# The lead of a transformer-layer kernel: products of ones on TensorE, and the second batch's first steps moved into it

## What is computed

```python
mod = (_silu(L0_c) @ L0_wmod).reshape(L0_c.shape[0], 6, 1, -1)
sa, ca, ga, sb, cb, gb = (mod[:, 0], mod[:, 1], mod[:, 2], mod[:, 3], mod[:, 4], mod[:, 5])
...
h = _layernorm(x, axis=-1) * (1 + ca) + sa
x = x + ga * _L0_attn_ref(h, L0_attn_wq, L0_attn_wk, L0_attn_wv, L0_attn_wo)
h = _layernorm(x, axis=-1) * (1 + cb) + sb
x = x + gb * _L0_ffn_ref(h, ...)
```

## Time and profile before

| | us |
|---|---|
| median of 3 runs | 591.85 |
| lowest, highest | 589.08, 592.23 |
| the profiled execution | 589.51 |
| its span, first to last instruction | 587.7 |
| the lead, up to the first scoreT (L876) | 48.1 |

### The profile page before, as it was taken

One profiled execution on the slowest core, in us unless ns is written; L12 is line 12 of the kernel. 1 busy time (PEld: TensorE's weight loads), 2 busy tenths in 40 slices (PEclk: granted clock), 3 DMA queues, 4 the chain that ended last, 5 costly groups with the idle time before them and its releaser, 6 DMA issues.

```text
span 587.7 us, 10308 instructions
## 1 busy us (share of the span) xinstructions
PE 556.5 (95%) x3102; PEld 308.3 (52%) x3102; DVE 371.3 (63%) x862; ACT 255.0 (43%) x519; POOL 206.6 (35%) x268
## 2 busy tenths in 40 slices
PE   4889999999999999999999999999999998999985
PEld 3453223233333333333443456557798897989664
DVE  6386577778678786788866359645344443433397
ACT  3213536664766647555477431103343443434100
POOL 6200000000030660306631753741666766666400
PEclk9976999999999999999999999999999999999998
DMA  7243117100221231311200588624455655542395
...
DMA packets 44004, 67.34 MB, mean 115 GB/s; under 512 B 9371, under 2 KB 32292, under 8 KB 43564
## 3 DMA queue, kind: packets, MB, share of 16 engines
...
## 4 chain that ended last, share of the span: by engine, by line
PE 81%; DVE 9%; issue 3%; DMA 3%; ACT 1%; POOL 1%; SPq 1%; POOLq 0%; ACTq 0%; DVEq 0%
PE ps L876 23%; PE ps L889 11%; PE ps L1107 8%; PE ps L973 7%; PE ps L1128 6%; PE ps L825 5%; PE ps L967 4%; PE ps L834 3%; PE ps L847 3%; PE ps L1093 3%; PE ps L902 3%; DVE max_q L1220 2%; PE ps L811 2%; DMA results<-y_sb,dest 1%; PE ps L932 1%
## 5 line engine op out<-in xcount | busy, mean ns | idle before, releaser
L1220 DVE TENSOR_REDUCE max_q<-ps 128x1 f32<-128x512 f32 x256 | 163.7, 685 | 71.5 <-PE ps L847 69.6
L703 ACT ACTIVATE probs<-ps 128x512 f32<-128x512 f32 x256 | 138.0, 596 | 100.8 <-PE ps L876 100.5
L847 PE MATMUL ps<-k_rows,q_rows 31*128 31x512 f32 x512 | 148.8, 673 | 2.0 <-DMA k_rows<-qk_raw 2.0
L876 PE MATMUL ps<-q_rows,k_rows 32*128 32x512 f32 x512 | 145.6, 647 | 0.9 <-DVE max_q L1220 0.9
L561 POOL DMA_INDIRECT results<-y_sb,dest x96 | 94.9, 989 | 67.0 <-issue 35.1
L876 PEld LDWEIGHTS ps<-q_rows,k_rows 32*128 32x128 f32 x512 | 41.8, 186 | 70.6 <-ACT probs L703 51.1
L1107 PE MATMUL ps<-up_sb,oT 128*128 x384 | 70.8, 327 | 2.3 <-DVE oT L1582 1.4
L889 PE MATMUL ps<-probs,v_ext 128*32 128x512 f32 x512 | 68.2, 605 | 1.1 <-ACT probs L703 1.1
L1107 PEld LDWEIGHTS ps<-up_sb,oT 128*128 128x128 f32 x384 | 61.3, 190 | 3.3 <-issue 3.2
L1128 PE MATMUL ps<-down_sb,e_hidT 96*128 x192 | 49.8, 382 | 3.6 <-ACT e_hidT L760 3.6
L1582 DVE COPY oT<-ps 128x512 f32<-128x512 f32 x48 | 33.0, 690 | 30.7 <-PE ps L1093 30.1
...
## 6 DMA issues: line engine op xcount, KB each, us to landing
...
```

What stands on the lines that cost most here:

```text
L703: act.activation(probs[:, u % 8, :], ps[:, st_bank(t.b, g, u), :], ACT.Exp).then_inc(exp_done, 1)
L847: pe.matmul(ps[:, banks[u % len(banks)], :], q_rows[32 * i:32 * i + ONE, b % 2, g, qt * P:(qt + 1) * P], k_rows[32 * i:32 * i + ONE, b % 2 ...
L876: pe.matmul(ps[:, st_bank(b, g, n), :], k_rows[32 * i:32 * i + 32, b % 2, g, kt * P:(kt + 1) * P], q_rows[32 * i:32 * i + 32, b % 2, g, :] ...
L1220: dve.tensor_reduce(max_q[:, g % 2, qt, i:i + 1], ps[:, banks[(16 * g + n) % len(banks)], :], AXX, ALU.max).then_inc(max_done, 1)
```

## The change

**Start.** PE begins with 14 products of ones by ones (of_ones), which only need the ones, now POOL's first instruction; two more stand after each of the first three column pairs of the modulation, and 8 after TP1. The results go to bank O and are never read. ACT's exp(-c) waits for c alone (c_ld). DVE clears half of q_rows, does the sigmoid, then the statistics; it normalises two of the four tiles (ACT the other two) and writes the second half of hT. POOL clears half of v_ext early, and k_rows and the other half after xn.

**Lead.** QK1's rows for group 0 are issued by ACT, not by SP. V0 is projected ahead of the first scores. Between the scores of the lead stand V1, 8 products of ones, the transposes of batch 1 (TP0+, TP1+), 4 products of ones; then QK0+ and QK1+ of batch 1, 8 products of ones, and 8 more after the last score. SP sends the maxima of group 0 ahead of the rest of wmod, and then places batch 1's first rows.

**Turn 0** loses TP0, TP1, QK0 and QK1 and has its other steps moved forward; places 7, 15, 23 and 29 are now empty.

```diff
--- before.py
+++ after.py
-    LEAD = ("TP0", "TP1", "QK0", "QK1", "QK2", "QK3", "V0", "V1", "MAX3")
-
-    FIRST = {"MAX0": 0, "TP0": 1, "TP1": 3, "QK0": 5, "QK1": 7, "MAX1": 8, "MOD0": 9, "MOD1": 11, "V0": (13, 15),
-             "MAX2": 16, "MODT": 17, "QK2": (19, 21), "QK3": (23, 25), "MAX3": 26, "V1": (27, 29), "NT0": 30, "NT1": 31}
+    LEAD = ("TP0", "TP1", "QK0", "QK1", "QK2", "QK3", "V0", "V1", "TP0+", "TP1+", "MAX3", "QK0+", "QK1+")
+
+    FIRST = {"MAX0": 0, "V0": (1, 3), "MOD0": 5, "MAX1": 8, "MOD1": 9, "QK2": (11, 13), "MAX2": 16, "MODT": 17, "QK3": (19, 21),
+             "MAX3": 24, "V1": (25, 27), "NT0": 30, "NT1": 31}
...
+    def done_in(self, lead):
+
+
+        for name, use in lead.uses.items():
+            if name.endswith("+"):
+                self.uses[name[:-1]] = use
...
+        c_ld, ones_s, v_clear, k_clear = (sem(n) for n in ("c_ld", "ones_s", "v_clear", "k_clear"))
...
+        turns[0].done_in(lead)
...
-            sp.dma_start(cT[:, :].rearrange("p (k b) -> p k b", k=KD), c_in.rearrange("(k p) b -> p k b", p=P)).then_inc(mod_ld, 16)
+            sp.dma_start(cT[:, :].rearrange("p (k b) -> p k b", k=KD), c_in.rearrange("(k p) b -> p k b", p=P)).then_inc(c_ld, 16)
...
             def turn(t):
                 max_rows(t, 0)
-                if t.pre:
+                if t.pre and not t.mod:
                     place_rows(t, 0, 0)
                     place_rows(t, 0, 1)
-                if t.mod:
-                    place_rows(t, 1, 0)
-                    place_rows(t, 1, 1)
                 max_rows(t, 1)
...
-            sp.wait_ge(consts, 3)
             sp.wait_ge(q_clear, 1)
+            place_rows(lead, 0, 0)
+            sp.wait_ge(q_clear, 2)
+            sp.wait_ge(k_clear, 1)
+            sp.wait_ge(v_clear, 2)
             sp.dma_start(k_rows[ONE:P:P // G, :, :, :].rearrange("p w g n -> p (w g n)"),
                          v_ext[0:G, :, :, :, :].rearrange("p w j h d -> p (w j h d)")).then_inc(ones_ld, 16)
-            for g in range(NG):
+            for g in range(1, NG):
                 for c in range(2):
                     place_rows(lead, 2 * (g // 2) + c, g)
+            max_rows(lead, 3)
             sp.dma_start(wmod[:, :, 2 * D:6 * D], wmod_in[:, 2 * D:6 * D].rearrange("(k p) n -> p k n", p=P)).then_inc(w_ld, 16)
             for w_d, w_s in ((wo, wo_sb), (gate, gate_sb)):
                 sp.dma_start(w_s[:, :, :], w_d.rearrange("(k p) n -> p k n", p=P)).then_inc(w_ld, 16)
-            max_rows(lead, 3)
+            for c in range(2):
+                for g in range(2):
+                    place_rows(turns[0], c, g)
             for w_d, w_s in ((sgate, sgate_sb), (sup, sup_sb), (sdown, sdown_sb)):
                 sp.dma_start(w_s[:, :, :], w_d.rearrange("(k p) n -> p k n", p=P)).then_inc(sh_ld, 16)
...
+            pool.memset(ones[:, :], 1.0).then_inc(ones_s, 1)
             st.did(pool.memset(ident[:, :], 0.0))
-            st.did(pool.memset(ones[:, :], 1.0))
...
+            pool.memset(v_ext[:, 0, :, :, :], 1.0).then_inc(v_clear, 1)
...
             deviations(0, TJ, 1)
-            pool.memset(v_ext[:, :, :, :, :], 1.0).then_inc(consts, 1)
-            pool.memset(k_rows[:, :, :, :], 0.0).then_inc(consts, 1)
+            pool.wait_ge(xn_ready, TJ)
+            pool.memset(k_rows[:, :, :, :], 0.0).then_inc(k_clear, 1)
+            pool.memset(v_ext[:, 1, :, :, :], 1.0).then_inc(v_clear, 1)
             deviations(TJ, NT, 2)
...
-            act.wait_ge(mod_ld, 32)
+            act.wait_ge(c_ld, 16)
             act.activation(ctmp[:, :], cT[:, :], ACT.Exp, scale=-1.0).then_inc(c_exp, 1)
...
             act.wait_ge(nmr_s, 1)
-            normalise(lead)
+            normalise(lead, range(2))
             act.wait_ge(modT_s, 1)
-            for k in range(KD):
-                to_hT(lead, f"TP{k}", 0)
-            for c in range(4):
-                raw_qk(lead, c)
-            for m in range(2):
-                values_out(lead, m)
-            negate_max(lead, 3)
+            to_hT(lead, "TP0", 0)
+            raw_qk(lead, 0)
+            raw_qk(lead, 1)
+            written(act, lead, "QK1")
+            act.wait_ge(k_clear, 1)
+            for i in range(G):
+                act.dma_start(k_rows[32 * i:32 * i + HD, 0, 0, :], qk_raw[32 * i:32 * i + HD, 1, :]).then_inc(rows_ld[0], 16)
+            raw_qk(lead, 2)
+            raw_qk(lead, 3)
+            values_out(lead, 0)
             act.wait_ge(nmr_s, 2)
             normalise(turns[0])
+            values_out(lead, 1)
+            for k in range(KD):
+                to_hT(turns[0], f"TP{k}", 1)
+            negate_max(lead, 3)
+            for c in range(2):
+                raw_qk(turns[0], c)
             for t in turns:
...
-            pe.wait_ge(mod_ld, 32)
+            def of_ones(times):
+
+
+                for n in range(times):
+                    pe.matmul(ps[:, O, 0:P], ones[:, :], ones[:, :], start=True, stop=True)
+
+            pe.wait_ge(ones_s, 1)
+            of_ones(14)
+            pe.wait_ge(mod_ld, 16)
             pe.wait_ge(c_ready, 1)
             for c in range(2 * KD):
                 for k in range(KD):
                     mm = pe.matmul(ps[:, 0, c * B:(c + 1) * B], wmod[:, k, c * P:(c + 1) * P], cT[:, k * B:(k + 1) * B],
                                    start=(k == 0), stop=(k == KD - 1))
+                if c < 2 * KD - 1:
+                    of_ones(2)
             mm.then_inc(modT_ps, 1)
             pe.wait_ge(consts, 1)
...
                     if b == 0 and u == 2:
-                        written(pe, lead, "V1")
+                        written(pe, lead, "QK0+")
                     above(pe, exp_done, 64 * b + u - 2)
...
             for k in range(KD):
                 tokens_to_columns(lead, f"TP{k}", 0)
+            of_ones(8)
             pe.wait_ge(qkv_ld, 48)
             for c in range(4):
                 project_qk(lead, c)
+            project_v(lead, 0)
             for n in range(16):
                 score(0, 0, n, SC + ST[0:2])
-                if n in (3, 7):
-                    project_v(lead, n // 4)
+                if n == 3:
+                    project_v(lead, 1)
+                if n == 7:
+                    of_ones(8)
+                if n == 11:
+                    for k in range(KD):
+                        tokens_to_columns(turns[0], f"TP{k}", 1)
+            of_ones(4)
             turn_max(lead, 3)
             for n in range(16):
                 score(0, 1, n, SC + ST[0:2])
+                if n in (3, 7):
+                    project_qk(turns[0], n // 4)
+                if n == 11:
+                    of_ones(8)
+            of_ones(8)
             pe.wait_ge(max_done, 32)
             pe.wait_ge(ones_ld, 16)
...
-            dve.memset(q_rows[:, :, :, :], 0.0).then_inc(q_clear, 1)
-            statistics(0, TJ)
-
+            dve.memset(q_rows[:, 0, :, :], 0.0).then_inc(q_clear, 1)
             dve.wait_ge(c_exp, 1)
             st.then(dve.tensor_scalar(ctmp[:, :], ctmp[:, :], 1.0, None, ALU.add))
             st.then(dve.reciprocal(ctmp[:, :], ctmp[:, :]))
+            dve.wait_ge(c_ld, 16)
             dve.tensor_tensor(cT[:, :], cT[:, :], ctmp[:, :], ALU.mult).then_inc(c_ready, 1)
+            statistics(0, TJ)
             minus_mean_over_deviation(0, TJ, 1)
+            dve.wait_ge(nmr_s, 1)
+            for j in (2, 3):
+                dve.tensor_scalar(xn[:, j, :], x[:, j * D:(j + 1) * D], rstd[:, j:j + 1], nmr[:, j:j + 1], ALU.mult, ALU.add).then_inc(xn_ready, 1)
             dve.wait_ge(modT_ps, 1)
-            st.then(dve.tensor_copy(modT[:, 0:KD * B], ps[:, 0, 0:KD * B]))
-            dve.tensor_scalar(modT[:, KD * B:], ps[:, 0, KD * B:2 * KD * B], 1.0, None, ALU.add).then_inc(modT_s, 1)
+            st.did(dve.tensor_copy(modT[:, 0:KD * B], ps[:, 0, 0:KD * B]))
+            st.then(dve.tensor_scalar(modT[:, KD * B:], ps[:, 0, KD * B:2 * KD * B], 1.0, None, ALU.add))
+            dve.sem_inc(modT_s, 1)
+            frees(dve.tensor_scalar(hT[:, 1, :], full(dve, lead, "TP1"), modT[:, (2 + 1) * B:(2 + 1) * B + 1], modT[:, B:B + 1], ALU.mult, ALU.add),
+                  lead, "TP1")
...
+            dve.memset(q_rows[:, 1, :, :], 0.0).then_inc(q_clear, 1)
             statistics(TJ, NT)
...
+            minus_mean_over_deviation(TJ, NT, 2)
             for n in range(16):
                 score_max(0, 0, n, SC + ST[0:2])
-            minus_mean_over_deviation(TJ, NT, 2)
             for n in range(16):
                 score_max(0, 1, n, SC + ST[0:2])
```

## The result

| us | before | after |
|---|---|---|
| median (4 runs each) | 591.79 (589.08 to 592.23) | **584.94** (584.11 to 585.91) |
| ratio after to before, 95% interval | | 0.990 (0.987 to 0.993) |
| the profiled execution; its span | 589.51; 587.7 | 584.85; 582.9 |
| first projection; first scores | 13.92; 24.50 | 13.15; 24.30 |
| first scoreT | 48.13 | 49.54 |

585.4 was forecast, 584.94 came; the sum, made against a profiled execution, gave 584.4, and the one of after took 584.85. The total hides three deviations, though: by these two traces the lead did not become 1.0 us shorter but 1.4 longer, turn 0 gave 4.8 instead of 4.1, and 1.4 us of the difference of the two spans arise after the turns, where the change touches nothing.

A forecast was written before the change was run, and what follows sets the result against it. DVE's row maxima were taken to pace the lead's scores, PE turn 0. Lead 1.0, turn 0 at full clock 2.1 and its moved steps 2.0 make 5.1 us off 589.51, 584.4; plus 1.0 gives 585.4 (8 in 10: 581.5 to 591).

The forecast's parts named there:

- The start: Lead up to first scores: ones raise PE's clock before the modulation, QK0 at 13.05 against 13.92; 2.1 us gained.
- four k rows, 4 x 0.63: Lead: ACT issues group 0's four k rows at 0.63 us each, to 19.8, landed at 21.8.
- the first scores at 22.4: Lead: first scores at 22.4 against 24.50, with V0 last; 2.1 us gained (1.3 to 2.8).
- The scores: Lead's scores: group 0 gains 0.15 us, the change of groups 0.4, group 1 with its new fillers loses 1.65.
- The clock's term: Turn 0's first places, MAX0 and TP0, at full clock: 2.1 us gained.
- The fillers' term: Turn 0 without TP0, TP1, QK0, QK1: 2.0 us gained (0 to 5.0), as empty places still wait 0.91.
- The sum: Whole kernel: 1.0 + 2.1 + 2.0 = 5.1 us off the profiled execution's 589.51, giving 584.4.
- (a): Rival, lead: the clock falls in spite of the ones, 10 us more, 595.4; chance 0.12.
- (b): Rival, start: ones don't raise the clock by the modulation, QK0 at 19.4, 6.3 us later, 591.7; chance 0.08.
- (c): Rival, turn 0: removing its four steps gives the full 5.0 us, 582.4; chance 0.10.
- (d): Rival: PE, not DVE, paces all 17 us at low clock; 8.5 us come back, not 2.5; 579.4; chance 0.03.
- (e): Rival: DVE's small steps give back turn 0's 2.0 us, ACT's issues hold V0 1.5 longer; 588.9; chance 0.10.

The follow-up runs named there:

- e4: Changed kernel with the ones row of k_rows copied early, as two DMAs ahead of group 0's q rows on SP: 582.73 us, 0.987 of before.
- e10: Changed kernel without any products of ones up to the first projection, those of the scores kept: 586.23 us in one execution.
- e6: Changed kernel once more, unchanged, for a second trace: 584.8 us (9 runs), 0.991 of before.
- e5: Kernel before once more, unchanged, for a second trace: 588.9 us (1 run).
- e7: Kernel before with only products of ones added in the lead's scores, nothing moved: 587.78 us, 0.996 of before.
- e3: Changed kernel with 8 products of ones added at each of turn 0's empty places 15, 23 and 29: 588.35 us, 0.996 of before.
- e2: Changed kernel without the products of ones between and behind the lead's scores, those of the start kept: 589.42 us, 0.996 of before.
- e9: Changed kernel with MOD0, MOD1 and MODT of turn 0 done in halves on two places each: 582.54 us, 0.986 of before.

## Why the prediction was right, and where it was not

**The start came out right up to QK0, in part by luck.** Ones before the modulation, the modulation at the fast pace, 3.3 us for it (3.2 forecast), QK0 at 13.15 (13.05). Two errors cancelled: PE could begin at 1.06 rather than 1.75 and was done with the ones at 6.4, but then it waited for wmod until 7.10. A third was hidden: the sigmoid was not done near 4.5 but at 5.57, since c landed at 4.2 and DVE's first step then took 0.65 us, and xn not by 9.6 but at 10.32. Had wmod landed at 6, QK0 would have come at 12.9 all the same, as in e4. The clock's rise within the ones was right: 28 instructions at 0.221 would be 6.2 us and took 5.36, and in e10 the projections were slow without them. Where in the ones it rises differs: they take from 4.74 us (e4) to 6.24 (e6).

**The step that failed is "four k rows, 4 x 0.63", and with it "the first scores at 22.4".** The four issues took 3.89 us, not 2.5, and the copy of QK2 behind them came at 21.36. I had named what is queued behind the issues but costed an issue by a row of before, where the same 64 KB transfer had been issued 2.7 us ahead of the first row (15.38 against 18.06) and not between the rows. e4 takes that transfer away and finds 22.32. Of the 2.1 us that the start was to give, 0.2 came (24.50 to 24.30; 1.0 by e5 and e6).

**The scores cost more than said.** From first scores to first scoreT it was 23.63 before and is 25.24: +1.6, where the sum had -0.15 - 0.4 + 1.65 = +1.1. Group 0 took 0.1 more than before (ones for V is an even swap, 0.65 behind them), the change of groups gave 0.42 (1.42 from the last maximum to the next against 1.84), and group 1 lost 1.95: the three idle times are 1.66, as forecast, and four separate groups of four maxima take 4 x 2.48 = 9.92, not 9.65.

**The clock's term was right,** 2.1 forecast and 1.9 to 2.4 by e7, which changes nothing else in turn 0. (The forecast's own terms, 6.06 us for the two places before less 3.83 less 0.3, come to 1.9 and not 2.1.) **The fillers' term too:** e7 and after both run turn 0 at the full clock and are 2.4 apart (76.3 and 73.9), against 2.0; e3 puts three of them back for 2.6.

**The sum.** The lead ends 1.41 us later, turn 0 is 4.80 shorter, so turn 1 begins 3.39 earlier:

```profile
126.86 0.27 ACT L614 ACTIVATE neg_max<-ps 16x128 f32<-16x128 f32 x1 [0.45 <-PE ps L855]
```

```profile
123.47 0.27 ACT L628 ACTIVATE neg_max<-ps 16x128 f32<-16x128 f32 x1 [0.45 <-PE ps L888]
```

These are that negation in before and in after. From here to the last MAX, both take 183.36 us, so the 3.4 are kept. The other 1.4 of the 4.8 between the spans arise in the experts' stretch and around it, and e5 shows the kernel before doing that by itself. So the change is worth 3.4 us where this pair of traces can see it, against 5.1 forecast; the other pairs, with e5 at 127.50 and e6 at 124.84, give 2.0 to 4.0. The forecast of the total was helped by chance: its sum had 1.7 us too much, 1.3 us that arise after the turns and outside the span went the same way (589.51 to 584.85 is 4.7), and of the 1.0 us added for the medians only 0.1 was needed on the side of after.

**The medians** are 5.7 to 6.9 apart, more than the traces. Each execution lists its mean granted clock. Over three comparisons the kernel before has 52 executions: 26 with a clock of 0.980 or more, median 589.4 us, and 26 below, median 591.9. Both profiled executions of it, at 0.982 and 0.979, took 589.5 and 588.9. The nine of e6 lie between 0.993 and 0.999. So slower executions of the kernel before go with a lower mean clock, and its traces, both among the fast ones, show no such execution. Whether it has further low spells, and where, stays open; a mean can't say it, since e5's lies under before's only by the tail beyond 550 us. e7 points the same way, though its interval is too wide to show it: 2.75 us by the medians (0.6 to 3.7), where the traces have 0.9 to 1.5 at turn 1's MAX0. So by the medians the change is worth more than its traces show, and the cause of that rest is not shown.

**The rivals.** (a), a fall in spite of the ones, did not come; e2 shows its mechanism where ones are missing. (b) did not come either. Of (c), turn 0 gave 4.8 rather than 5.0 + 2.1, so it is out. (d) is out by e7. Of (e), one half, ACT's issues holding back V0, came in full (2 us where 1.5 was said) and the other, DVE setting turn 0's pace, did not until e9.
